# Spreading inverse degrees by two DMAs instead of TensorE, with the incidence products moved forward

## What is computed

```
h = relu(layernorm(x));  x = x + L0(h, adj)
L0:  H = (adj != 0);  w = first row of adj
     Dn = H @ w;              Dn = where(Dn > 0, 1/Dn, 0)     # a degree per node
     Be = sum of H over nodes; Be = where(Be > 0, 1/Be, 0)
     conv(v) = Dn * (H @ (Be * (H.T @ v)))
     y = conv(layernorm(relu(conv(h @ W1) + b1)) @ W2) + b2;  return y + h
h = relu(layernorm(x));  x = x + L1(h, adj)      # graph attention
h = relu(layernorm(x));  x = x + L2(h, adj)      # three-hop transition, weights Wv, Wk
h = relu(layernorm(x));  x = x + L3(h, adj)      # query/key sums, softmax over nodes
```

## Time and profile before

| | |
|---|---|
| median of 3 runs | 1412.56 us (1412.31 to 1417.0) |
| span of the profiled execution | 1411.1 us |
| TensorE matmul busy | 1367.8 us, 97% |
| TensorE weight loads, beside the matmuls | 1249.5 us, 89% |
| VectorE | 1271.7 us, 90% |
| ScalarE | 1053.6 us, 75% |
| GpSimd | 946.2 us, 67% |
| DMA queue of SP, share of 16 engines | 13.7% |
| transposes of `deg`, busy | 20.2 us, 128 of 283 ns |

### The profile page before, as it was taken

One profiled execution on the slowest core, in us unless ns is written; L12 is line 12 of the kernel. 1 busy time (PEld: TensorE's weight loads), 2 busy tenths in 40 slices (PEclk: granted clock), 3 DMA queues, 4 the chain that ended last, 5 costly groups with the idle time before them and its releaser, 6 DMA issues.

```text
span 1411.1 us, 33599 instructions
## 1 busy us (share of the span) xinstructions
PE 1367.8 (97%) x8954; PEld 1249.5 (89%) x8954; DVE 1271.7 (90%) x5267; ACT 1053.6 (75%) x2345; POOL 946.2 (67%) x972
## 2 busy tenths in 40 slices
PE   7789999999999999999999999999999999999986
PEld 6678999999999999999999999999999999999975
DVE  6879999999999999999999999999999999999884
ACT  4557777877777887777887777787777788777764
POOL 5657766667766666766666776666786666676533
PEclk9899999999999999999999999999999999999999
DMA  4000111101111101111110111110111111111001
GB/s 127 31 31 23 39 39 54 54 23 45 52 39 50 52 29 43 47 52 37 52 47 27 45 52 37 52 52 22 45 52 45 44 52 35 39 45 37 31 31 53
DMA packets 75384, 62.16 MB, mean 44 GB/s; under 512 B 3013, under 2 KB 70985, under 8 KB 75338
## 3 DMA queue, kind: packets, MB, share of 16 engines
q1 hardware_dynamic: 75338, 61.63, 13.7%
HBM read 36.45 MB, written 16.78 MB: 38 GB/s over the span
## 4 chain that ended last, share of the span: by engine, by line
PE 92%; DVE 5%; issue 2%; ACT 1%; POOL 0%; DMA 0%; DVEq 0%; ACTq 0%; POOLq 0%
PE ps L371 39%; PE ps L356 25%; PE ps L375 20%; PE ps L477 4%; PE ps L432 3%; DVE stats L1590 1%; DVE prod L1774 1%; PE ps L633 0%; DVE h L1602 0%; DVE x L1737 0%; PE ps L629 0%; DVE x L1685 0%; DVE z L1730 0%; DMA adj_f<-in_adjT 0%; DVE el L1675 0%
## 5 line engine op out<-in xcount | busy, mean ns | idle before, releaser
L1315 POOL TENSOR_TENSOR x3n<-p,x 128x512 f32<-128x512 f32 x63 | 80.9, 1284 | 259.8 <-ACT p L982 259.8
L1275 POOL TENSOR_TENSOR hT_lo<-hT,hT_hi 128x512 fp32r<-128x512 f32 x126 | 161.3, 1302 | 57.0 <-ACT hT L924 42.1
L1255 POOL TENSOR_TENSOR rs<-var_e,neg_half 128x4 f32<-128x4 f32 x160 | 165.2, 1033 | 23.7
L903 ACT ACTIVATE p<-ps,rs 128x256 f32<-128x256 f32 (+1 forms) x256 | 136.6, 597 | 29.1 <-DVE sij L1691 28.8
L371 PE MATMUL ps<-wl_hi,h2T_hi 128*128 128x512 f32 (+1 forms) x512 | 149.1, 373 | 0.7 <-DVE x L1737 0.7
L356 PE MATMUL ps<-p,alT 128*128 128x256 f32 (+1 forms) x512 | 142.9, 382 | 0.5 <-DVE p L1715 0.5
L371 PE MATMUL ps<-wl_lo,h2T_hi 128*128 128x512 f32 (+1 forms) x512 | 132.8, 341 | 0.0
L375 PE MATMUL ps<-wl_hi,h2T_lo 128*128 128x512 f32 (+1 forms) x512 | 132.2, 340 | 0.0
L1590 DVE BATCH_NORM_STATS2 stats<-x 128x6 f32<-128x256 f32 x256 | 108.8, 425 | 5.7
L1000 ACT ACTIVATE h3T_hi<-ps 128x512 fp32r<-128x512 f32 x64 | 38.3, 598 | 91.0 <-PE ps L477 87.1
L924 ACT ACTIVATE hT_hi<-ps,cols_sb 128x512 fp32r<-128x512 f32 x128 | 87.4, 683 | 21.7 <-PE ps L375 21.5
(11 more groups left out here) (192 smaller groups left out, 4607.8 us busy)
## 6 DMA issues: line engine op xcount, KB each, us to landing
x_in<-in_x SPq DMA_DIRECT2D x32, 512.0 KB, 3.5
out_x<-x SPq DMA_DIRECT2D x32, 512.0 KB, 3.2
adj_f<-in_adjT SPq DMA_DIRECT2D x32, 256.0 KB, 2.8
adj_m<-in_adjT SPq DMA_DIRECT2D x32, 256.0 KB, 2.9
adj_l<-adj_m SPq DMA_DIRECT2D x32, 256.0 KB, 2.4
vqk<-in_l_wk SPq DMA_DIRECT2D x3, 256.0 KB, 4.6
x<-in_w1T SPq DMA_DIRECT2D x1, 512.0 KB, 6.7
x<-in_w2T SPq DMA_DIRECT2D x1, 512.0 KB, 7.7
```

The lines of the kernel that those rows point to most:

```text
L903: return act.activation(dst, src, ACT.Copy, scale=scale)
L1255: pool.tensor_tensor(rs[:, layer, :], var_e[:, layer, :], neg_half[:], ALU.pow).then_inc(done, G)
L1275: pool.tensor_tensor(hTs[1][:, hc, :], hT[:, hc, :], hTs[0][:, hc, :], ALU.subtract).then_inc(S["hT_lo"], 1)
L1315: pool.tensor_tensor(x3n[:, s], p0[:, s], x2[:, s], ALU.add).then_inc(S["x3_ready"], 2)
```

## The change

From round 1 on the row of inverse degrees no longer passes TensorE. SP writes the column `deg[:, 2, :]` as a row of 512 numbers to DRAM, waits for it, and loads this row into all 128 partitions of `deg_sp`; `next_gt` reads it from there. The first two groups (rounds -1 and 0, `early`) keep the old way. `next_s` moves forward on TensorE, from between the third and fourth `front_c2` to behind `front_sums`, and its banks become 7 and 5; `copy_s` moves forward on ScalarE with it and takes the degree's column along; `next_degrees` moves forward on VectorE, from between `front_residual(1)` and its statistics to ahead of `late_low(0)`. Waits follow the banks.

```diff
@@ buffers and banks
+        deg_row = nc.dram_tensor("deg_row", [1, G * C], F32, kind="Internal").ap()
+        deg_sp = sb("deg_sp", G, C)
-        s_sb = sb("s_sb", G, C)
+        s_sb = sb("s_sb", G, C + 1)
-        "s": (3, 4), "d": (2,), "c2": (5, 0),
+        "s": (3, 4), "s2": (7, 5), "d": (2,), "c2": (5, 0),
+        def early(r):
+            return not r.steady and r.i < 1
@@ SP
             def load_adj(r):
                 wait(sp, S["pen_ready"], r.front(G))
+                wait(sp, S["gt_ready"], r.front(G))
+            def spread_degrees(r):
+                sp.wait_ge(S["deg_ready"], r.next(G))
+                with nc.allow_non_contiguous_dma(reason="a column of four becomes a row"):
+                    sp.dma_start(deg_row.rearrange("a (g p) -> p (a g)", g=G), deg[:, 2, :]).then_inc(S["rd_stored"], 16)
+                sp.wait_ge(S["rd_stored"], r.loads(r.i - 1))
+                sp.dma_start(deg_sp[:].rearrange("p g c -> p (g c)"),
+                             deg_row.broadcast_to((P, G * C))).then_inc(S["rd_loaded"], 16)
                 if past.has_front:
                     load_mask(past)
+                if r.has_next:
+                    spread_degrees(r)
@@ TensorE
             def next_s(r, b):
-                if b == 0:
-                    wait(pe, S["z_ready"], r.front(G))
+                if early(r):
+                    if b == 0:
+                        wait(pe, S["z_ready"], r.front(G))
+                elif b == 0:
+                    wait(pe, S["p2_copied"], r.mid(G))
                 elif b == 1:
-                    wait(pe, S["zb_ready"], r.mid(G))
+                    wait(pe, S["p2_copied"], r.mid(2))
             def late_h3(r, b):
                 if b == 0:
                     wait(pe, S["p2_copied"], r.mid(2))
+                    if r.has_next:
+                        wait(pe, S["s_copied"], r.next(G))
             def mid_p10(r, g):
                 elif g == 1:
                     wait(pe, S["p2_copied"], r.mid(G))
+                    if r.has_next:
+                        wait(pe, S["s_copied"], r.next(2))
             def mid_ap(r, g):
                 if g == 0:
-                    if not r.steady and r.i == 1:
-                        wait(pe, S["deg_ready"], r.next(G))
+                    wait(pe, S["zb_ready"], r.mid(G))
             def late_vqk(r, g):
                 if g == 0:
-                    wait(pe, S["deg_ready"], r.next(G))
+                    wait(pe, S["z_ready"], r.front(G))
             def body(r):
                     front_sums(r, 3)
+                if r.has_next:
+                    next_s(r, 0)
+                    next_s(r, 1)
                 if r.has_mid:
                     mid_b2(r)
...
                     front_c2(r, 2)
-                if r.has_next:
-                    next_s(r, 0)
-                    next_s(r, 1)
-                if r.has_front:
                     front_c2(r, 3)
...
                     mid_ap(r, 0)
-                if r.has_next:
-                    next_d(r)
-                if r.has_mid:
                     mid_ap(r, 1)
@@ ScalarE
             def body(r):
                     copy_p2(r, 3)
+                if r.has_next:
+                    copy_s(r, 0)
+                    copy_s(r, 1)
                 if r.has_late:
                     copy_h3T(r, 0)
...
                     norm_x(r, 0)
-                    copy_s(r, 0)
-                    copy_s(r, 1)
                     norm_x(r, 1)
@@ VectorE
             def next_gt(r):
                 dve.wait_ge(S["s_copied"], r.next(G))
-                dve.wait_ge(S["rd_spread"], r.next(G))
-                dve.tensor_tensor(gt[:], bank("d").rearrange("p (g c) -> p g c", g=G), s_sb[:],
-                                  ALU.mult).then_inc(S["gt_ready"], G)
+                if early(r):
+                    dve.wait_ge(S["rd_spread"], r.next(G))
+                    rows_of = bank("d").rearrange("p (g c) -> p g c", g=G)
+                else:
+                    dve.wait_ge(S["rd_loaded"], r.loads(r.i - 1))
+                    rows_of = deg_sp[:]
+                dve.tensor_tensor(gt[:], rows_of, s_sb[:, :, 0:C], ALU.mult).then_inc(S["gt_ready"], G)
             def body(r):
                     tail_norm(r)
+                if r.has_next:
+                    next_degrees(r)
                 if r.has_late:
                     late_low(r, 0)
...
                     front_residual(r, 1)
-                if r.has_next:
-                    next_degrees(r)
-                if r.has_front:
                     front_ln1(r, 1)
```

More of the change, by code:

```diff
@@ L213, in gnn_stack @@
         st0 ag0 h0_ready var0 rs0_ready xb_ready
-        s_ready s_copied deg_a deg_b deg_ready rd_spread gt_ready nm0 nmr_ready res0_ready
+        s_ready s_copied deg_a deg_b deg_ready rd_spread rd_stored rd_loaded gt_ready nm0 nmr_ready res0_ready
         yT_ready yT_copied yT_lo u_ready hT_ready hT_hi hT_lo sq_step sq_half sq_done hsums_ready zr_ready hst_ready hm_a hvar_ready vare_h rsh_ready z_ready
@@ L224, in gnn_stack @@
         S = {n: sem(n) for n in names}
-        BANK = {"u": (1, 2, 0, 3), "y": (1, 4), "s": (3, 4), "d": (2,), "c2": (5, 0), "b1": (0, 3), "att": (3, 5),
+        BANK = {"u": (1, 2, 0, 3), "y": (1, 4), "s": (3, 4), "s2": (7, 5), "d": (2,), "c2": (5, 0), "b1": (0, 3), "att": (3, 5),
                 "h2": (7, 6), "p2": (4, 5, 6, 7), "p10": (6, 7, 5, 0), "b2": (4,), "z": (0, 1, 2, 3),
@@ L235, in bank_pair, with s_bank @@
             return ps[:, BANK[name][g // 2], (g % 2) * D:(g % 2 + 1) * D]
+        def early(r):
+            return not r.steady and r.i < 1
+        def s_bank(r):
+            return "s" if early(r) else "s2"
         def logits(b):
@@ L420, in next_s @@
             def next_s(r, b):
-                if b == 0:
-                    wait(pe, S["z_ready"], r.front(G))
+                if early(r):
[3 more added lines that the diff above has]
+                    wait(pe, S["p2_copied"], r.mid(G))
                 elif b == 1:
-                    wait(pe, S["zb_ready"], r.mid(G))
+                    wait(pe, S["p2_copied"], r.mid(2))
                 for g in (2 * b, 2 * b + 1):
                     pe.wait_ge(S["binc_ready"], r.next(g + 1))
-                    product(bank("s", b)[:, (g % 2) * (C + 1):(g % 2 + 1) * (C + 1)],
+                    product(bank(s_bank(r), b)[:, (g % 2) * (C + 1):(g % 2 + 1) * (C + 1)],
                             lambda c: inc_T[:, g, :], lambda c: binc_T[:, g, :], 1).then_inc(S["s_ready"], 1)
@@ L499, in mid_p10 @@
                     wait(pe, S["p2_copied"], r.mid(G))
+                    if r.has_next:
+                        wait(pe, S["s_copied"], r.next(2))
                 elif g == 2:
                     wait(pe, S["x1_ready"], r.front(2))
+                    if not r.steady and r.i == 1:
+                        wait(pe, S["s_copied"], r.next(G))
                     if not r.steady and r.i == GROUPS:
@@ L975, in copy_s @@
                 act.activation(s_sb[:, 2 * b:2 * b + 2, :],
-                               bank("s", b)[:, 0:2 * (C + 1)].rearrange("p (g c) -> p g c", g=2)[:, :, 0:C],
+                               bank(s_bank(r), b)[:, 0:2 * (C + 1)].rearrange("p (g c) -> p g c", g=2),
                                ACT.Copy).then_inc(S["s_copied"], 2)
@@ L1020, in centre_logits @@
             def centre_logits(r, b):
+                if b == 1:
+                    wait(act, S["p10_copied"], r.mid(1))
                 centre(1, x1, bank("hp", b).rearrange("p (g d) -> p g d", g=2), b, r.front, S["nm1_ready"], S["hp_ready"], 2 * b)
@@ L1640, in degrees @@
             def degrees():
-                b = BANK["s"]
-                return (ps[:, b[0]:b[1] + 1:b[1] - b[0], 0:2 * (C + 1)]
-                        .rearrange("p b (g c) -> p b g c", g=2)[:, :, :, C])
+                return s_sb[:, :, C]
             def degree_bounds(r):
                 dve.wait_ge(S["s_copied"], r.next(G))
-                dve.tensor_scalar(deg[:, 0, :].rearrange("p (b g) -> p b g", b=2), degrees(), TINY, None,
+                dve.tensor_scalar(deg[:, 0, :], degrees(), TINY, None,
                                   ALU.max).then_inc(S["deg_a"], G)
@@ L1655, in degree_masked @@
                 dve.wait_ge(S["deg_b"], r.next(G))
-                dve.scalar_tensor_tensor(deg[:, 2, :].rearrange("p (b g) -> p b g", b=2), degrees(), 0.0,
-                                         deg[:, 1, :].rearrange("p (b g) -> p b g", b=2), ALU.is_gt,
+                dve.scalar_tensor_tensor(deg[:, 2, :], degrees(), 0.0, deg[:, 1, :], ALU.is_gt,
                                          ALU.mult).then_inc(S["deg_ready"], G)
```

## The result

The changed kernel takes 1587.38 us (median of 4, 1582.61 to 1591.91) against 1412.43 us of the kernel before: a ratio of 1.1228, 95% interval 1.1198 to 1.1257. The forecast was 1419.2 us, with a range to 1434. What came is the rival "the row comes late", which had a chance of 0.08 and a price of 1452.

What follows compares the result with a forecast made beforehand. TensorE was taken to bound the kernel, provided VectorE delivers on time. Four waits, 0.26 + 0.17 + 0.12 + 0.11, less 0.44 saved, gave +0.22 us a round, thirty times +6.6: 1419.2 us, range 1406 to 1434.

Steps and rivals of the forecast that it cites:

- the row comes late: Rival: store and load together exceed 10.9 us, so `gt` and VectorE behind it stand; 12 us would give 1452; chance 0.08.
- price the pair at nothing: Store and load of the row: bounds 6.4 to 10.7 us, the lower taken, against 10.9 us available; no cost.
- the 10.9 us of air: Time from the column leaving at about 666.9 us to `gt` wanting the row at 677.8.
- A microsecond late is about a microsecond a round: Price of a late row at `gt`: each microsecond of lateness lengthens the round by about as much.
- `gt` reads SBUF instead of PSUM ... nothing to under 0.1 us: VectorE's product `gt` with its row operand moved to SBUF: a cost of nothing to under 0.1 us.
- 0.44 us of TensorE in a round ... 13.2 us at most: Saving from dropping the four degree transposes on TensorE: 0.44 us a round, thirty rounds, 13.2 us at most.
- the third of my four waits: TensorE waiting for VectorE's `wh12`, after the saved transposes: 0.12 us a round.
- The waits of the moved order: New TensorE waits caused by moving products and degrees, without the transposes' saving: 0.66 us a round.
- The first of them, 0.26 us at `late_h3`: TensorE waiting at `late_h3`'s first half for ScalarE to copy the incidence products out of bank 5: 0.26 us.
- the second, 0.17 for the residual: TensorE waiting at `mid_p10(3)` for VectorE's second residual: 0.17 us a round.
- The fourth, for `p1`: TensorE waiting at `next_y(1)` for VectorE's first `mid_z1`: 0.11 us a round.
- VectorE becomes the loop: Rival: VectorE reaches `elu_low` late, all lateness added, +0.4 to +0.8 us a round, 1424.6 to 1436.6; chance 0.13.

Runs made afterwards that it cites:

- e3: The changed kernel with the column stored as 128 pieces of 16 bytes instead of 512 of 4, `gt` reading the row with a stride: 1474.29 us.
- e5: The changed kernel with no row made and no transfers, `gt` taking one source from PSUM bank 2 (output not the reference's): 1430.53 us.
- e2: The changed kernel without both transfers, `gt` multiplying by a constant in SBUF in place of the row: 1465.14 us.
- e9: The kernel before, order and banks untouched, without the four transposes from round 1 on, `gt` taking its factor from PSUM bank 2: 1411.28 us.
- e4: The changed kernel's order and banks, but the row spread by TensorE's four transposes as before, no transfers: 1432.63 us.
- e11: The changed kernel with 16-byte store pieces, ScalarE copying the row to PSUM, `h3` transposes before the incidence products, second `h3T_lo` before `gt`: 1451.05 us.
- e8: The changed kernel storing 128 adjacent 4-byte pieces, loading 512 bytes per partition, nobody waiting for the row, `gt`'s factor from PSUM: 1431.30 us.
- e6: The changed kernel with both transfers and the wait for the row, but `gt` taking its factor from PSUM bank 2: 1535.78 us.

## Why the prediction was wrong

**The step that failed: "I take the lower end, as nothing else is under way there, and price the pair at nothing."** The 6.4 us were twice the time of an output store, whose 512 pieces are of 1 KB; it stood for a store of 4-byte pieces, and for the load as well. Measured from issue to issue and from the load's issue to `gt`, the pair takes 9.05 + 5.33 = 14.4 us, more than the other bound that I had written, 10.7, too. That one alone left only 0.2 of the 10.9 us of air, so the late row should have weighed far more than the 0.08 of the rival. The place, `gt`, and the engine were the rival's. e3 shows that it is the store's shape: with pieces of 16 bytes the row is in time.

**"A microsecond late is about a microsecond a round"** was too little: by it the 3.5 us beyond the air would give 1419.2 + 105 = 1524 us. The row is 14.57 - 11.23 = 3.34 us late against e5. With 0.23 us for the longer `gt`, that leaves 47.67 - 42.63 - 3.57 = 1.47 us a round; TensorE's busy time, for the same products, is 1421.9 - 1376.5 = 45.4 us longer than in e5, 1.51 a round. That is the low clock after the stops, as the trace of the change shows within itself. Three of its rounds got no low clock; here is one of them and the round behind it, which had it for 3.4 us (length, busy PE, PEld, DVE, ACT, POOL, granted clock):

```profile
505.80:552.03 46.23, 42.32 (x278) 38.07 (x275) 39.77 (x164) 32.93 (x73) 29.47 (x31) 1.00 0.15 45
552.03:599.68 47.65, 43.67 (x278) 39.29 (x275) 39.27 (x163) 32.91 (x73) 29.44 (x31) 0.96 0.14 44
```

The three are 46.2 us long, most of the others 47.7.

**"`gt` reads SBUF instead of PSUM ... nothing to under 0.1 us"** failed as well: 1.07 us a round where the row is in time (e2 against e5). In the change most of it lies under the wait.

**"0.44 us of TensorE in a round ... 13.2 us at most"**: the length is right, its worth is not. In the order of before it is 1.7 us (e9), in the moved order 2.1 (e5 against e4), since behind it TensorE waits for VectorE: in e5 its weight loads stand 10.0 us ahead of the transposes of `wh` (1.3 in e4) and 14.2 for the second `h3T_lo` ahead of `mid_ap(3)` (6.5 in e4). The first of these is the third of my four waits, 0.26 us in the round read where I had 0.12. The second was not among the four: I followed `wh12` and `p1` out of VectorE's late chain, but not bank 7.

**The waits of the moved order**, +0.66 a round without the credit, were nearly right: e4, which still has the transposes, measured +0.77. The first of them, 0.26 us at `late_h3`, shows in e4 as 7.1 us in 25 waits, 0.28 each, and the second, 0.17 for the residual, as 6.9 us of the weight loads in 31 waits, 0.22 each:

```profile
PE ps L499 <- ACT s_sb L999: 7.1, 25, 0.3
```

```profile
PEld ps L388 <- DVE x L1761: 6.9, 31, 0.4
```

The fourth, for `p1`, shows in e4 and e5 in two rounds only.

e4 and e5 lie in the range of the rival "VectorE becomes the loop", 1424.6 to 1436.6, but that is luck, as its sign did not come: VectorE idles ahead of `elu_low` as it did before (`el`; the kernel before, then e5).

```profile
DVE el L1675 <- PE ps L375: 11.5, 28, 0.4
```

```profile
DVE el L1702 <- PE ps L392: 12.2, 28, 0.4
```

What is full is a shorter stretch of VectorE, between its two `h3T_lo`. In e5:

```profile
674.70 0.69 DVE L1508 SCALAR_TENSOR_TENSOR h3T_lo<-ps,h3T_hi 128x512 fp32r<-128x512 f32 x1 [0.86 <-ACT h3T_hi L1021]
685.55 0.68 DVE L1508 SCALAR_TENSOR_TENSOR h3T_lo<-ps,h3T_hi 128x512 fp32r<-128x512 f32 x1
```

VectorE goes from its first `h3T_lo` at 674.70 to the second at 685.55, 10.85 us; in before from 666.52 to 677.94, 11.42, with the degrees (0.54) in between. It waits for no other engine in either. But the stretch begins 3.31 us after the column sums' end (671.39) instead of 1.86 after 664.66, as the transposes of `h3` now stand behind the incidence products and their copies: 1.45 us later, less 0.57.

So a round of the change is 41.89 + 0.77 (order and banks) - 0.03 (transposes) + 3.34 (late row) + 0.23 (`gt`) + 1.47 (what is left, for the clock) = 47.67.

## What to carry to other kernels

Bound an unseen transfer by a row of its own shape, piece size and layout included; where one of its two ends all but uses up the air there is, as here 10.7 of 10.9 us, the late case is a main case and not a tail. Before crediting time taken off the busiest engine, look for the next wait behind it and ask how much air that has: here none, and 13 us were worth 2. When an operand moves from PSUM to SBUF, count the SBUF sources of the instruction and look at what GpSimd does then; a longest time far above the median, like that of `wh`, is the sign, and the degree operation of e11 shows that one source can be enough.

## What the runs showed of the hardware

- 4-byte pieces that lie side by side in DRAM: 7.1 us for 128 and 8.5 to 11 us for 512; with gaps between them 1.4 and 2.7 us. 128 pieces of 16 bytes side by side: 1.4 us.
- The load of one row of 2 KB to 128 partitions took 3.9 us alone (e3) and 5.3 to 5.5 with the load of `x` issued 1.1 us behind it; 512 bytes to each partition took 5.1 us, with that load behind it as well (e8), so a quarter of the bytes hardly shortens it.
- A 128x512 product of VectorE with both sources in SBUF took 1.76 us where it met an addition of GpSimd, 0.69 with one source in PSUM; a 128x4 `TENSOR_SCALAR` with one source, in SBUF, took 1.07 instead of 0.17 (e11).
- After a stop of 4 us TensorE's granted clock was 0.50 in the 2.7 us that followed, in all but three of the rounds; the thirty stops cost 45 us of longer products beside their own length. In e6, with stops of 2.7 us, about every second round had such a stretch: rounds with it took some 47.0 us, rounds without 45.1.
